# Four graph layers in one kernel: edge bucketing moved from GpSimd's scatter to TensorE, counts and gcn passes in bfloat16 pieces

## What is computed

```
h = max(layernorm(x), 0)                             # before each of the four layers
sage:  n = segment_sum(w * h[src], dst); out = h @ Ws.T + n @ Wn.T; x += out / |out|
gcn:   twice: out = dinv * (C^T + I) (dinv * (h @ W)) + b, a relu between; C counts edges, deg = in-degree + 1
hop:   twice: h' = 0.5 * norm_adjacency(w) h + 0.5 * h0;  x += relu(h') @ W.T + b
rel:   twice: segment_sum(relu((h @ W[type])[src] + b), dst)
```

## Time and profile before

| | us |
|---|---|
| median of 3 runs | 2972.81 |
| lowest and highest | 2971.26, 2975.32 |
| span of the profiled execution | 2974.7 |
| PE busy | 2562.7 (86%) |
| DVE busy | 1254.7 (42%) |
| POOL busy | 1291.0 (43%) |
| ACT busy | 537.0 (18%) |

### The profile page before, as it was taken

One profiled execution on the slowest core, in us unless ns is written; L12 is line 12 of the kernel. 1 busy time (PEld: TensorE's weight loads), 2 busy tenths in 40 slices (PEclk: granted clock), 3 DMA queues, 4 the chain that ended last, 5 costly groups with the idle time before them and its releaser, 6 DMA issues.

```text
span 2974.7 us, 37615 instructions
## 1 busy us (share of the span) xinstructions
PE 2562.7 (86%) x11805; PEld 2031.2 (68%) x11806; DVE 1254.7 (42%) x2688; ACT 537.0 (18%) x1584; POOL 1291.0 (43%) x1271
## 2 busy tenths in 40 slices
PE   4699999999799999999999999588888876666666
PEld 3488888888799998888777776355555544444444
DVE  4888888888321442111233333233333422222222
ACT  0255555555200000000111112111111110000000
POOL 2787777770000000000000000577777747777776
PEclk9899999999899999999999999799989987787787
DMA  2033333333398774444444443444545443333333
GB/s 92 4 136 136 132 125 133 137 137 135 136 297 297 244 244 153 150 150 154 132 137 139 141 145 104 150 147 146 160 146 160 146 129 110 109 111 109 111 109 94
DMA packets 168353, 426.05 MB, mean 143 GB/s; under 512 B 39048, under 2 KB 102646, under 8 KB 168082
## 3 DMA queue, kind: packets, MB, share of 16 engines
q1 hardware_dynamic: 57052, 258.59, 25.2%
q0 software_dynamic: 53248, 109.98, 13.4%
q10 hardware_dynamic: 57910, 55.64, 5.4%
HBM read 284.37 MB, written 139.73 MB: 143 GB/s over the span
## 4 chain that ended last, share of the span: by engine, by line
PE 60%; POOL 25%; issue 9%; DVE 3%; DMA 1%; ACT 1%; SPq 1%; PEldq 0%; DVEq 0%; POOLq 0%; PEld 0%; ACTq 0%
PE agg L880 28%; POOL gathered L635 25%; PE y L767 9%; PE agg L788 9%; PE y L726 7%; PE prod L719 3%; PE agg L927 1%; PE turn_ps L704 1%; SPq L459 1%; DMA gathered<-in_edge_weight 1%; PE y L685 1%; DMA gathered<-table_rel,idx_rel 0%; PE y L681 0%; PE y L719 0%; DVE stream L1215 0%
## 5 line engine op out<-in xcount | busy, mean ns | idle before, releaser
L635 POOL DMA_INDIRECT gathered<-table_rel,idx_rel x832 | 797.1, 958 | 1493.1 <-DMA table_rel<-gathered 1240.2
L927 PE MATMUL agg<-gathered,onehot 128*128 x2048 | 594.7, 453 | 283.5 <-SPq L554 212.9
L927 PEld LDWEIGHTS agg<-gathered,onehot 128*128 128x128 f32 x2048 | 454.1, 227 | 427.8 <-issue 353.2
L880 PE MATMUL agg<-t_sb,stream 128*128 128x128 f32 (+1 forms) x3750 | 563.2, 312 | 14.7 <-issue 7.8
L598 POOL DMA_INDIRECT edges_bucketed<-edges,pos_u x416 | 488.6, 1174 | 175.9 <-issue 124.1
L880 PEld LDWEIGHTS agg<-t_sb,stream 128*128 128x128 f32 x3750 | 526.3, 193 | 48.6 <-issue 15.2
L1577 DVE SCALAR_TENSOR_TENSOR onehot<-iota,tilebase,edges 128x256 f32<-128x256 f32 x512 | 243.4, 485 | 721.2 <-PE agg L927 697.3
L767 PE MATMUL y<-gathered,relw 128*128 128x256 f32 x1300 | 336.0, 382 | 14.6 <-ACT gathered L1032 12.1
L788 PE MATMUL agg<-h_sb,stream 128*128 128x257 f32 x1250 | 320.4, 381 | 0.0
L767 PEld LDWEIGHTS y<-gathered,relw 128*128 128x128 f32 x1300 | 246.5, 191 | 49.8 <-ACT gathered L1032 15.2
L973 ACT COPY turned<-turn_ps 128x256 f32<-128x256 f32 (+2 forms) x100 | 39.8, 398 | 1301.6 <-PE turn_ps L704 1300.0
(11 more groups left out here) (157 smaller groups left out, 1497.2 us busy)
## 6 DMA issues: line engine op xcount, KB each, us to landing
table_rel<-y_sb ACTq DMA_DIRECT2D x176, 256.0 KB, 3.3
stream<-counts_dense SPq DMA_DIRECT2D x50, 832.0 KB, 4.6
stream<-weights_dense SPq DMA_DIRECT2D x50, 832.0 KB, 4.4
stream<-counts_dense SPq DMA_DIRECT2D x50, 768.0 KB, 4.4
stream<-weights_dense SPq DMA_DIRECT2D x50, 768.0 KB, 4.4
weights_dense<-stream SPq DMA_DIRECT2D x25, 832.0 KB, 3.4
counts_dense<-t_sb SPq DMA_DIRECT2D x25, 832.0 KB, 5.1
weights_dense<-stream SPq DMA_DIRECT2D x25, 768.0 KB, 5.1
```

What stands on the lines that cost most here:

```text
L635: pool.indirect_dma_start(gathered[:, slot * D:(slot + 1) * D], None, tables[n], bass.IndirectOffsetOnAxis(ap=idx_rel[:, c:c + 1], axis=0) ...
L880: mm = pe.matmul(sums(n, t)[:, 0:width], stream[:, at % 2, s * P:(s + 1) * P], table(n, s), start=s == 0, stop=s == TILES - 1)
L927: mm = pe.matmul(agg[b][:, 0:width], onehot[:, half_ * QUAD + k, :], gathered[:, bass.ds((q & (GQ - 1)) * (QUAD * D) + k * D, width)], sta ...
```

## The change

The scatter through DRAM goes, with its prefill and SP's loads of records. In its place each edge gets five fields in bfloat16, local source and destination number plus one and the weight in three pieces (`fields_of_edges`, on POOL). For every tile DVE makes two one-hots for the chunks that can hold its edges (up to 25): of the bucket (26 wide) and of the slot (128 wide) (`slots_of`). POOL multiplies the bucket one-hots with the five fields (`value_buckets`). TensorE multiplies the slot one-hots with the result, 130 columns per chunk, and so puts each edge in its bucket and slot (`permute`). DVE copies the result from PSUM and adds the weight pieces (`take_tile`).

In the build the 256-column f32 product is split into one f32 product of 128 columns for the weights and one bfloat16 product of 128 for the counts, which reads the upper half of the f32 one-hots. The degrees are taken by one-column bfloat16 products for each bucket, and DVE's reductions go. Counts are stored in bfloat16. gcn1 and gcn2 read them in whole tiles through a ring of four, and multiply with tables of three bfloat16 pieces side by side (384 columns), with a product with the identity for the loop. DVE adds the three parts and splits the next table; the first table is split by POOL (`split`). Edge loads are in 96, 7 and 1 rows, weights and types on ACT's queue. The tables of hop1 and hop2 change places, and three tiles of relation rows have rows of their own instead of four and two.

```
+    def window(t):
+        return max(0, E * t // N - MARGIN), min(CHUNKS, -(-E * (t + 1) // N) + MARGIN)
...
-    WIDTH = {"gcn1": HID, "gcn2": HID, "hop1": D, "hop2": D, "rel1": D, "rel2": D}
+    WIDTH = {"gcn1": 3 * HID, "gcn2": 3 * HID, "hop1": D, "hop2": D, "rel1": D, "rel2": D}
...
-        c_dram = dram("counts_dense", (NPAD, NPAD))
+        c_dram = dram("counts_dense", (NPAD, NPAD), BF16)
...
+        PIECES = 3
+        pieces = {n: of[:, 0:PIECES * LANE // 2].bitcast(BF16).rearrange("p (t k d) -> p t k d", k=PIECES, d=HID)
+                  for n, of in (("gcn1", t_sb), ("gcn2", gathered))}
+        counts = [stream[:, k % 2, (k // 2) * LANE // 2:(k // 2 + 1) * LANE // 2].bitcast(BF16) for k in range(RING)]
...
+        def load_edges(eng, a, to, done):
+            for lo, hi in ((0, 96), (96, QP - 1)):
+                eng.dma_start(to[lo:hi, :], a[lo * F:hi * F].rearrange("(q e) -> q e", e=F)).then_inc(done, 16)
+            eng.dma_start(to[QP - 1:QP, 0:E - (QP - 1) * F],
+                          a[(QP - 1) * F:E].rearrange("(q e) -> q e", q=1)).then_inc(done, 16)
...
-            bucketed = recs_dram.rearrange("(p c) f -> p c f", p=P)
...
-                    last = sp.value_load(bounds[BOUNDS:P, i + 1:i + 2], min_val=0, max_val=QUADS - 1)
-                    sp.wait_ge(scat_landed, last + 1)
...
-                    sp.dma_start(recs[:, i % RECS, :, :], bucketed[:, i * BCK:(i + 1) * BCK, :]
-                                 ).then_inc(s_rec[i % RECS], 16)
...
+                        sp.dma_start(counts[at % RING], c_dram[t * P:(t + 1) * P, :]).then_inc(s_count[at % RING], 16)
...
-                    pool.indirect_dma_start(
-                        recs_dram, bass.IndirectOffsetOnAxis(ap=pos_u[0:rows, c:c + 1], axis=0),
...
+            def value_buckets(t):
+                lo, hi = window(t)
+                wide = hi - lo
+                pool.wait_ge(slots_ready, t + 1)
+                nc.gpsimd.tensor_tensor(valued[:, 0:wide, :, :],
+                                        bucket_hot[:, 0:wide, :].unsqueeze(2).broadcast_to([P, wide, FIELDS, BCK]),
+                                        fields[:, lo:hi, :].unsqueeze(3).broadcast_to([P, wide, FIELDS, BCK]), ALU.mult
+                                        ).then_inc(values_ready, 1)
+            def split(n, to, t, k):
+                pool.wait_ge(whole_ready, k + 1)
+                made(nc.gpsimd.tensor_copy(pieces[to][:, t, 0, :], whole))
+                made(nc.gpsimd.tensor_tensor(remains, whole, pieces[to][:, t, 0, :], ALU.subtract))
+                made(nc.gpsimd.tensor_copy(pieces[to][:, t, 1, :], remains))
+                made(nc.gpsimd.tensor_tensor(remains, remains, pieces[to][:, t, 1, :], ALU.subtract))
+                made(nc.gpsimd.tensor_copy(pieces[to][:, t, 2, :], remains))
+                pool.sem_inc(S[n, "table_ready"], 1)
+            fields_of_edges()
+            for t in range(TILES + 6):
+                if t < TILES:
+                    value_buckets(t)
+                if t >= 6:
+                    split("sage", "gcn1", t - 6, t - 6)
...
+            def upper(of):
+                return of.bitcast(BF16).rearrange("p (d two) -> p d two", two=2)[:, :, 1]
...
+                first = True
                 for k, s in enumerate(GROUPS[part][group]):
-                    buckets = [s - lo] + [hi - lo] * (s == t)
-                    for j, bucket in enumerate(buckets):
-                        mm = pe.matmul(bank[:, k * D:(k + 1) * D], src_hot[:, h % 2, bucket, :],
-                                       pair_hot[:, h % 2, bucket, :, :].rearrange("p k d -> p (k d)"),
-                                       start=j == 0, stop=j == len(buckets) - 1)
+                    for at_ in [s - lo] + [hi - lo] * (s == t):
+                        pe.matmul(bank[:, k * D:k * D + P], src_hot[:, h % 2, at_, :], pair_hot[:, h % 2, at_, 0, :],
+                                  start=first, stop=True, skip_group_check=True)
+                        first = False
+                        mm = pe.matmul(bank[:, k * D + P:(k + 1) * D], upper(src_hot[:, h % 2, at_, :]),
+                                       upper(pair_hot[:, h % 2, at_, 1, :]), start=False, stop=True,
+                                       skip_group_check=True)
                 mm.then_inc(built, 1)
-            def degrees(t):
-                pe.wait_ge(sum_made, 2 * t + 2)
-                for k in range(2):
-                    pe.matmul(sums("sage", t)[:, D + 1:D + 2], hot_sum[:, (2 * t + k) % 4, :], ones[:, 0:1],
-                              start=False, stop=True, skip_group_check=True)
+            def degrees(h):
+                t, part = h // 2, h % 2
+                lo, hi = PARTS[part]
+                if part == 0:
+                    pe.wait_ge(sum_free, t + 1)
+                    pe.wait_ge(perm_read, min(t + 2, TILES))
+                buckets = hi - lo + (lo <= t < hi)
+                for at_ in range(buckets):
+                    mm = pe.matmul(sums("sage", t)[:, DEG:DEG + 1], upper(pair_hot[:, part, at_, 1, :]), ones_b[:, 0:1],
+                                   start=part == 0 and at_ == 0, stop=True, skip_group_check=True)
+                mm.then_inc(deg_done, 1)
+            def permute(t):
+                lo, hi = window(t)
+                pe.wait_ge(slots_ready, t + 1)
+                pe.wait_ge(values_ready, t + 1)
+                if t >= 3:
+                    pe.wait_ge(sum_free, t)
+                for c in range(hi - lo):
+                    mm = pe.matmul(perm_ps[t % 2], slot_hot[:, c, :], valued[:, c, :, :].rearrange("p f s -> p (f s)"),
+                                   start=c == 0, stop=c == hi - lo - 1, skip_group_check=True)
+                mm.then_inc(permuted, 1)
...
+            permute(0)
+            permute(1)
             for i in range(2 * (TILES - 1) + 9):
                 left = [((i - 1) // 2, s) for s in range(*PARTS[(i - 1) % 2])] if 1 <= i <= HALVES else []
                 if i < HALVES:
                         left = left[2:]
                 for t, s in left:
                     sage_sum(t, s)
+                if i < HALVES:
+                    degrees(i)
                 if i % 2:
-                    if i < HALVES:
-                        degrees(i // 2)
+                    if (i + 3) // 2 < TILES:
+                        permute((i + 3) // 2)
...
+                        if part == 1 and n in ("gcn1", "gcn2"):
+                            mm = pe.matmul(sums(n, t)[:, 0:width], ident_b[:], table(n, t), start=False, stop=True,
+                                           skip_group_check=True)
...
+            act.wait_ge(s_pad, 1)
+            load_edges(act, edge_weight, flat_w, s_edge)
+            load_edges(act, edge_type, flat_i[:, 2 * F:3 * F], s_edge)
...
+            def slots_of(t):
+                lo, hi = window(t)
+                wide = hi - lo
+                prep(nc.vector.scalar_tensor_tensor(own_slot[:, 0:wide], tile_b[:, lo:hi], float(t), slot1[:, lo:hi],
+                                                    ALU.is_equal, ALU.mult))
+                if t >= 1:
+                    dve.wait_ge(permuted, t)
+                nc.vector.tensor_tensor(bucket_hot[:, 0:wide, :],
+                                        bucket[:, lo:hi].unsqueeze(2).broadcast_to([P, wide, BCK]),
+                                        iota[:, 0:BCK].unsqueeze(1).broadcast_to([P, wide, BCK]), ALU.is_equal)
+                nc.vector.tensor_tensor(slot_hot[:, 0:wide, :],
+                                        iota1[:].unsqueeze(1).broadcast_to([P, wide, P]),
+                                        own_slot[:, 0:wide].unsqueeze(2).broadcast_to([P, wide, P]), ALU.is_equal
+                                        ).then_inc(slots_ready, 1)
+            def take_tile(t):
+                rec = recs[:, t % RECS, :, :]
+                if t >= RECS:
+                    dve.wait_ge(dw_ready, 2 * (t - RECS) + 2)
+                dve.wait_ge(permuted, t + 1)
+                prep(nc.vector.tensor_copy(rec.rearrange("p f s -> p (f s)"), perm_ps[t % 2]))
+                dve.sem_inc(perm_read, 1)
+                prep(nc.vector.tensor_tensor(rec[:, 2, :], rec[:, 2, :], rec[:, 3, :], ALU.add))
+                prep(nc.vector.tensor_tensor(rec[:, 2, :], rec[:, 2, :], rec[:, 4, :], ALU.add))
...
-            for what in ("src", "dst", "sum"):
+            dve.wait_ge(s_fields, 1)
+            slots_of(0)
+            take_tile(0)
+            slots_of(1)
+            for what in ("src", "dst"):
                 onehots(0, what)
             for i in range(2 * (TILES - 1) + 9):
                 ahead = i + 1 < HALVES
+                if i % 2 == 0:
+                    if (i + 2) // 2 < TILES:
+                        take_tile((i + 2) // 2)
+                    if (i + 4) // 2 < TILES:
+                        slots_of((i + 4) // 2)
                 if ahead:
                     onehots(i + 1, "src")
```

(14 more changed lines are left out.)

297 lines of the change are left out of this document (150 added, 147 removed).

## The result

The changed kernel takes 3184.32 us (median of 4 runs, 3182.87 to 3184.91) against 2974.07 us for the kernel before, a ratio of 1.0704 with a 95% interval of 1.0689 to 1.0719. The forecast was 3052 us with a range of 2945 to 3150. The direction was right, the size was not: +210 us instead of +79, and the time lies above the range.

The account below looks back on a forecast made before the run. The build runs at TensorE's rate; DVE's new block would stall it. Front -11, build +105, clock +34, gcn1 -35, fetch -3, gcn2 -11 make +79 on 2974.7: 3052 us, range 2945 to 3150 (its own 2995 to 3100).

Parts of the forecast that it names:

- What bounds the build: Build: now TensorE's rate, DVE close behind; afterwards DVE's 11.1 us before its first eviction's end stalls TensorE 6.1 us a tile.
- VectorE's block ahead of the first eviction: Start of each even half: new DVE work queued before evictions, 11.1 us from the permutation's end to the first eviction's end.
- cover: TensorE's turns and three build groups before it needs a bank back: 5.0 us of work while DVE is late.
- pricing POOL's product at nothing for VectorE: Build: the forecast sum added no DVE delay from POOL's multiplication of bucket one-hots with fields.
- rival 2: Build: POOL's product stops DVE steps with two SBUF operands, 1.5 to 6 us in 20 tiles; 3082 to 3172 us; 25%.
- TensorE's work: Build: 23.2 us of TensorE work a tile, 2.1 less than before the change.
- second stall: Build: ACT's late weighing of the next half frees a bank at 16.9 us, TensorE wants it at 15.7: 1.2 us.
- rival 1: Build: TensorE isn't held up, 25 x -2.1 us and no clock loss; 2860 us, milder form 2910; 17%.
- The clock: Build: TensorE's clock drops after idles, 1.7 us lost for each 6 us stall, 20 tiles: +34 us (0 to 60).
- The front: Before the first build: faster edge loads -28 us, added work after the ranking +17 us, together -11 us.
- The added chain: Between ranking and first build: one-hots, POOL's field product, 21 matmuls, copy, next one-hots: +17 us (13 to 18).
- gcn1 and gcn2: Dense passes: gcn1 tiles 4.2 us, -35 us; shorter idle before gcn2, -3; gcn2 tiles 6.3 us by DVE's loop, -11.

## Why the prediction was wrong

**What bounds the build: right.** VectorE's block ahead of the first eviction became what TensorE waits for, at the place and for the reason given. In 7 of the 14 tiles the eviction that ends the wait is VectorE's and in 7 it is ScalarE's, whose roots had waited for VectorE's steps, as forecast. From the end of the permutation at 616.8 to the end of the first eviction at 633.4 are 16.6 us. The prediction's 11.1 us and the hold of 5.45 (7.40 less 1.95) make that sum. Its parts were right as well: 3.48 us for the slot one-hots (3.4 forecast), 5.3 us of cover (5.0).

**The step that failed: pricing POOL's product at nothing for VectorE.** The prediction said that no row decides whether the product stops VectorE, gave it 25%, and took the sum without it. The mechanism came as rival 2 described it, 5 us a tile and nothing that covers it; fills, copies and the move of the product to VectorE confirm it. What should have decided is that the rule which the prediction quotes from the Trainium skill named the case, a step with two SBUF inputs beside a GpSimd instruction that reads, and that nothing in the trace stood against it. Absence of a row was treated as evidence for zero. With the hold of 120 us on top of the forecast the sum is 3172 us, the upper end of rival 2's own bounds (3082 to 3172). The last 12 us are the balance of the other terms. By tile: forecast 23.2 + 6.1 + 1.2 + 1.7 = 32.2 us, measured 25.1 of work, 1.7 of clock and 11.1 of waiting, 37.8 us; so 5.0 us are the hold, 1.9 TensorE's work, and the second stall takes 1.2 off.

**TensorE's work: mis-sized.** 23.2 us a tile were forecast. With the products in the changed kernel's order, at a clock of nearly 1.00, it is 25.1 busy (the run with early source one-hots), and 24.3 with the other order and fewer evictions. Most of the difference is the 13 groups at 1.54 instead of 1.43 us, 1.4 us a tile; the rows of the two orders put 0.06 us of each 0.11 on one f32 product behind a bfloat16 one. It also ends rival 1: a build that never waits would gain 0.2 to 1 us a tile, not 2.1. (The 1.0 us is with the other order of products; with the changed kernel's own it is 0.2.) The kernel with fewer evictions, which is nearest to rival 1, takes 653.0 us from its first build (145.51) to gcn1 (798.55), against 654.1 before: its whole gain of 62 us comes from gcn1 and gcn2.

**The second stall of 1.2 us: wrong.** No idle of its own shows behind the long one: from 633.41 to 650 us TensorE is busy throughout. It works at a granted clock of 0.53 until 637.40 and so reaches the bank later; that this alone hides the stall is not shown. The 15.7 us at which the prediction has TensorE want the bank is also not worked out there.

**The clock: right in size.** 1.7 us of loss for each stall were forecast. TensorE is busy for 26.8 us a tile against 25.1 for the same instructions at nearly full clock, 1.7 us, in spite of a stall twice as long as the 6 us it was meant for. In the run with the block moved, which has 3.5 us of idle time a tile in place of 11.1, it is busy for 26.7 us, 1.6 more than 25.1. So the loss did not grow with the idle time, and that the price for a stall of 6 us fits here is partly luck.

**The front: two terms.** The loads brought the first build forward by the 28 us forecast, as the run with them alone shows. In the changed kernel TensorE ends the ranking 22 us earlier, not 28. Part of the 6 us is again the hold: while GpSimd makes the fields, VectorE's small steps of the ranking are late. These two rows of VectorE (0.18 us each in the kernel with three fields) stand beside GpSimd steps from 26.05 to 28.56 us:

```profile
26.15 1.05 DVE L1301 CAST stream<-stream 128x32 int32<-128x32 f32 x1
27.24 1.36 DVE L1302 TENSOR_SCALAR stream<-stream 128x32 int32<-128x32 int32 x1
```

With three fields, hence three GpSimd steps fewer, the ranking ends at 105.7 instead of 111.8; that is more than the late steps that I can name, so the rest stays open. The added chain was 21 us instead of 17 (the parts that the prediction lists for it add up to 16.3); the one-hots of tile 0 were held for 5.4 us in it, one of the 24 holds.

**gcn1 and gcn2: right.** A gcn1 tile takes 4.23 us (4.2 forecast). A gcn2 tile takes 6.11 us, bound by VectorE's loop as described (6.3 forecast); two rows a tile apart, to be read beside the earlier trace rows:

```profile
1199.81 0.42 DVE L1622 TENSOR_TENSOR x_sb<-prod,x_sb 128x256 f32<-128x256 f32 x1 [1.04 <-PE prod L769]
...
1205.92 0.42 DVE L1622 TENSOR_TENSOR x_sb<-prod,x_sb 128x256 f32<-128x256 f32 x1 [1.03 <-PE prod L769]
```

The extra gain of 13 us in both passes against the forecast lies mostly in their starts: gcn2 begins without any idle (4.47 before), its first two tiles take 4.2 us each instead of 7.1, and gcn1 no longer waits 3.37 us behind its first products, 13.6 us together where the forecast had 3. Some 3 us more are gcn2's tile of 6.11 instead of 6.3 us.

## What to carry to other kernels

Work moved to a near-idle GpSimd is free only if VectorE does nothing beside it that needs the same way into memory: look at which VectorE instructions stand behind the one that starts GpSimd, and price the whole GpSimd instruction when one of them has two inputs in SBUF or is a tensor_scalar or cast. Cutting that instruction up shortens each hold, but every piece has its own cost and can be held itself: five pieces paid here, thirteen did not. Where a block of new work stands in an engine's list can be worth more than its length: the same instructions behind the fourth and fifth groups instead of ahead of the first took 170 us less. And where a known rule names exactly the case at hand and no row speaks against it, it belongs in the sum, not among the rivals.

## What the hardware showed

- GpSimd reading memory holds VectorE's two-input steps and its f32 tensor_scalar of 2 or more columns, for whole instructions; one-column tensor_scalars (0.15 us) and copies out of PSUM (0.42 us) passed beside the product unhindered.
- A GpSimd instruction that only writes (1.8 us fills) held the two-column tensor_scalar and not the two-input one-hot.
- The hold works in both directions. The product of 3,250 elements took 5.64 us alone, 7.08 behind a VectorE one-hot, 9.75 in five pieces and 13.25 in thirteen; of the last, 4.4 us were waits for VectorE and 3.2 us the cost of twelve more instructions.
- An f32 build product behind a bfloat16 one cost TensorE about 0.06 us (0.28 us start to start instead of 0.22); an f32 turn with shorter weight loads (141 ns instead of 193) behind a bfloat16 product did not.
- After a wait of 11.3 us TensorE was granted a clock of 0.53 for some 4 us and 1.00 behind them; the loss was 1.7 us a tile.
